# A graph layer's edge loop: one TensorE signal a step instead of four, and relu(h1) ahead of relu(h2)

## The reference

```python
msg_in = jnp.concatenate([node_features[row], node_features[col]], axis=-1)
h = jax.nn.relu(msg_in @ Wm1 + bm1)          # h1, 256 wide
h = jax.nn.relu(h @ Wm2 + bm2)               # h2, 256 wide
messages = h @ Wm3 + bm3
agg = jax.ops.segment_sum(messages, col, num_segments=num_nodes)
...
agg = agg / jnp.clip(count, 1.0)[:, None]
upd = jax.nn.relu(jnp.concatenate([node_features, agg], axis=-1) @ Wn1 + bn1) @ Wn2 + bn2
x = _layernorm(x + (node_features + upd), axis=-1)
```

## Time and profile before

| what | value |
|---|---|
| time, median of 3 runs | 1221.72 us |
| span of the profiled execution | 1422.7 us |
| stage 1, up to the first transpose of the loop | 89 us |
| edge loop in the profiled execution | 1236 us, 391 steps |
| stage 3 in the profiled execution | 97.7 us |
| mean granted TensorE clock | 0.991 |

### The profile page before, as it was taken

One profiled execution on the slowest core, in us unless ns is written; L12 is line 12 of the kernel. 1 busy time (PEld: TensorE's weight loads), 2 busy tenths in 40 slices (PEclk: granted clock), 3 DMA queues, 4 the chain that ended last, 5 costly groups with the idle time before them and its releaser, 6 DMA issues.

```text
span 1422.7 us, 34295 instructions
## 1 busy us (share of the span) xinstructions
PE 1256.0 (88%) x9586; PEld 1169.5 (82%) x9587; DVE 969.2 (68%) x2072; ACT 728.3 (51%) x1392; POOL 772.3 (54%) x814
## 2 busy tenths in 40 slices
PE   6978988888889988998889888999888988899897
PEld 5868888888888888888888888888888888888786
DVE  6856666666666666666666766767676776777676
ACT  3544554554554554554555454545545445455585
POOL 2166666666666665666666656666656666664000
PEclk9999999999999999999999999999999999999999
DMA  9765555455444545555445545454554445555012
GB/s 303 284 222 153 144 146 147 146 146 148 144 147 143 149 147 146 145 145 147 147 144 146 149 144 146 143 150 142 145 147 144 144 144 147 147 143 151 15 65 87
DMA packets 135603, 211.39 MB, mean 149 GB/s; under 512 B 24247, under 2 KB 102669, under 8 KB 134030
## 3 DMA queue, kind: packets, MB, share of 16 engines
q1 hardware_dynamic: 98030, 108.43, 25.5%
q0 software_dynamic: 37536, 102.55, 24.7%
HBM read 188.09 MB, written 22.80 MB: 148 GB/s over the span
## 4 chain that ended last, share of the span: by engine, by line
PE 58%; issue 16%; DVE 6%; another core or an unknown queue 6%; ACT 5%; DVEq 4%; DMA 2%; POOL 1%; SPq 1%; ACTq 0%
PE bank L1407 27%; PE bank L1365 9%; PE bank L1311 5%; PE sums L1328 4%; ACT bank L728 2%; PE sums L1332 2%; PE bank L1438 2%; PE sums L1336 2%; PE sums L1334 2%; ACT h L731 2%; PE sums L1451 1%; DVE h_lo L1098 1%; DVE onehot_t L1013 1%; DVE h L1104 1%
## 5 line engine op out<-in xcount | busy, mean ns | idle before, releaser
L624 POOL DMA_INDIRECT a_edge<-a_table,src_idx x782 | 752.9, 963 | 479.8 <-remote 280.5
L1407 PE MATMUL bank<-w,h 128*128 128x256 f32 x4692 | 655.4, 283 | 93.7 <-issue 92.6
L1407 PEld LDWEIGHTS bank<-w,h 128*128 128x128 f32 x4692 | 595.6, 189 | 116.7 <-issue 116.2
L721 ACT ACTIVATE h_hi<-bank 128x512 fp32r<-128x512 f32 x391 | 234.6, 600 | 453.3 <-remote 360.6
L1098 DVE SCALAR_TENSOR_TENSOR h_lo<-bank,h_hi 128x512 fp32r<-128x512 f32 x391 | 267.6, 685 | 137.5 <-issue 132.5
L1104 DVE SCALAR_TENSOR_TENSOR h<-bank,h 128x512 fp32r<-128x512 f32 x391 | 268.3, 686 | 105.9 <-ACT h L731 53.5
L731 ACT ACTIVATE h<-bank 128x512 fp32r<-128x512 f32 x391 | 234.1, 599 | 135.5 <-remote 62.2
L1365 PE MATMUL bank<-ident,a_edge 128*128 128x128 f32 x1564 | 241.8, 277 | 35.7 <-DVE onehot_t L1013 18.8
L1028 DVE SCALAR_TENSOR_TENSOR onehot<-iota,first_node,dst_col 128x256 fp32r<-128x256 int16 x391 | 187.4, 479 | 88.0 <-issue 86.5
L728 ACT COPY bank<-b_bc 128x512 f32<-128x512 f32 x391 | 234.8, 600 | 23.5 <-DVE h_lo L1098 17.4
L1365 PEld LDWEIGHTS bank<-ident,a_edge 128*128 128x128 f32 x1564 | 177.8, 141 | 54.2 <-DVE onehot_t L1013 30.7
(11 more groups left out here) (186 smaller groups left out, 668.5 us busy)
## 6 DMA issues: line engine op xcount, KB each, us to landing
b_win<-b_table SPq DMA_DIRECT2D x391, 128.0 KB
rel<-rel_dram SPq DMA_DIRECT2D x196, 128.0 KB
a_edge<-a_table,src_idx POOLq DMA_INDIRECT x782
a_table<-work SPq DMA_DIRECT2D x12, 512.0 KB, 4.8
b_table<-work SPq DMA_DIRECT2D x5, 1024.0 KB
b_table<-h SPq DMA_DIRECT2D x4, 1024.0 KB
f_x<-in_x SPq DMA_DIRECT2D x12, 256.0 KB, 6.0
b_table<-a_edge SPq DMA_DIRECT2D x3, 1024.0 KB, 6.1
```

Of the source, the lines that this page charges most:

```text
L624: pool.indirect_dma_start(a_edge[:, b % R * TB + t, :], None, a_table, bass.IndirectOffsetOnAxis(ap=src_idx[:, b * TB + t:b * TB + t + 1], ...
L721: act.activation(h2_hi[:, (k - AHEAD - 1) % U, :, 0:H], bank[H2[(k - AHEAD - 1) % U]][:, :].rearrange("p (t h) -> p t h", t=TB), ACT.Relu) ...
L1407: ins = pe.matmul(to, h1[:, j, a, h * EB + t * P:h * EB + (t + 1) * P], w2[:, b, h, :], start=False, stop=(a == 1 and h == KH - 1), skip_g ...
```

## The change

It does four things. (1) TensorE no longer raises `s_ta`, `s_sg` and `s_w2` in each step; `s_ex`, behind the expansion, is the one signal of a step, and the order of TensorE's queue makes it stand for the transposes of the same step and for the sums and the W2 products of the step before. In the last steps, where no expansion follows, `s_w2` (the last 3) and `s_sg` (the last 6) are still raised. GpSimd now waits for `s_ex`. (2) ScalarE computes relu(h1) of step k first, then puts b2, then computes relu(h2) of step k - 3 (LAG = 3) without a wait of its own. VectorE follows the same order: low part of h1, one-hot for step k + 2, then the one-hot and the low part of h2 of step k - 3. (3) VectorE adds a finished range one step later. (4) On TensorE the branch for further ranges moves from ahead of the expansion to ahead of `begin_range`.

```diff
-                    pool.wait_ge(s_ta, b - R + 1)
+                    pool.wait_ge(s_ex, b - R + 1)
...
 # ScalarE
                 for k in steps(i):
-                    if there(i, k - AHEAD - 1):
-                        act.wait_ge(s_w2, i * U + (k - AHEAD))
-                        act.activation(h2_hi[...], bank[H2[(k - AHEAD - 1) % U]], ACT.Relu).then_inc(s_h2h, 1)
                     if there(i, k):
+                        if isinstance(i, int) and U * i + k < LAG:
+                            put_b2(k)
+                        act.wait_ge(s_ex, i * U + (k + 1))
+                        act.activation(h1[:, k % U, 0, :], bank[k % 2][:, :], ACT.Relu).then_inc(s_h1h, 1)
                         if there(i, k - U):
                             act.wait_ge(s_h2l[k % U], nth(i, k - U))
-                        act.copy(bank[H2[k % U]][:, :], b2_bc)
-                        act.wait_ge(s_ex, i * U + (k + 1))
-                        act.activation(h1[:, k % U, 0, :], bank[k % 2][:, :], ACT.Relu).then_inc(s_h1h, 1)
+                        if not isinstance(i, int) or U * i + k >= LAG:
+                            put_b2(k)
+                    if there(i, k - LAG):
+                        if among_last(i, k - LAG, LAG):
+                            act.wait_ge(s_w2, nth_last(i, k - LAG, LAG))
+                        act.activation(h2_hi[...], bank[H2[(k - LAG) % U]], ACT.Relu).then_inc(s_h2h, 1)
...
 # VectorE, end_range
-                dve.wait_ge(s_sg, i * U + (k + 1))
+                if among_last(i, k, BACK + 1):
+                    dve.wait_ge(s_sg, nth_last(i, k, BACK + 1))
...
 # VectorE: the pair of step k - 3 (make_onehot, h2_lo) moves behind h1_lo(k) and make_onehot_t(k + 2);
-                            with dve.If((word & 2**8) > 0):
-                                end_range(i, k - BACK, word)
+                            with dve.If((word & 2**8) > 0):
+                                end_range(i, k - BACK - 1, word)
...
 # TensorE
-                        ins.then_inc(s_ta, 1)
-                    with pe.If((word & (2**13 - 1)) > 0):
-                        (further ranges of k - BACK - 1; far spans of k)
+                        spans = word & 127
+                        with pe.If(spans > 0):
+                            with pe.Fori(1, within(spans, 1, NFE) + 1):
+                                expand_far(k)
                         expand(b_win[:, k % RB, :], onehot_t[:, k % 2, :], k).then_inc(s_ex, 1)
...
                             with pe.If(word > 2**13 - 1):
+                                sum_all_further(k - BACK - 1, word)
                                 begin_range(k - BACK)
...
-                        other_sums(bank_at(own), (k - BACK) % U, k - BACK).then_inc(s_sg, 1)
+                        ins = other_sums(bank_at(own), (k - BACK) % U, k - BACK)
+                        if among_last(i, k - BACK, BACK + 1):
+                            ins.then_inc(s_sg, 1)
...
-                        ins.then_inc(s_w2, 1)
+                        if among_last(i, k - AHEAD, LAG):
+                            ins.then_inc(s_w2, 1)
```

More of the change, by code:

```diff
@@ L24 @@
 BACK = 5
+LAG = AHEAD + 1
 XB = 7
@@ L269, in gnn_layer @@
         s_h1l = [sem(f"s_h1_lo{k}") for k in range(U)]
-        s_w2 = sem("s_h2_product")
+        s_w2 = sem("s_last_h2_product")
         s_bits = sem("s_banks_written")
@@ L277, in gnn_layer @@
         s_wrap = sem("s_edges_wrapped")
-        s_sg = sem("s_segments_summed")
+        s_sg = sem("s_last_segments_summed")
         s_sgm = sem("s_further_segments_summed")
@@ L398, in there, with among_last, nth_last @@
             return not isinstance(i, int) or 0 <= U * i + k < NBE
+        def among_last(i, k, n):
+            return isinstance(i, int) and U * i + k >= NBE - n
+        def nth_last(i, k, n):
+            return U * i + k - (NBE - n) + 1
         def steps(i, back=BACK):
@@ L627, in _ @@
                                             ).then_inc(s_g[b % R], 16)
-            pool.wait_ge(s_w2, NBE)
+            pool.wait_ge(s_w2, LAG)
             for k in range(2):
@@ L712, in load_far, with put_b2 @@
                                       ).then_inc(s_bf, 16)
+            def put_b2(k):
+                act.copy(bank[H2[k % U]][:, :], b2_bc[:, :, :].rearrange("p t h -> p (t h)"))
             def body(i):
@@ L1091, in body @@
                             make_far_onehot_t(0, j)
-                for k in steps(i, BACK + 1):
+                for k in steps(i, BACK + 2):
                     word = words[k]
[L1094 to L1098, removed]
-                                                 bank[H2[j]][:, :].rearrange("p (t h) -> p t h", t=TB),
-                                                 0.0, h2_hi[:, j, :, 0:H].bitcast(F32),
-                                                 ALU.max, ALU.subtract).then_inc(s_h2l[j], 1)
                     if there(i, k):
@@ L1346, in sum_further, with sum_all_further @@
                 other_sums(bank_at(other), FURTHER, k).then_inc(s_sgm, 1)
+            def sum_all_further(k, word):
+                further = (word >> 7) & 63
+                with pe.If(further > 0):
+                    with pe.Fori(1, within(further, 1, NW - 1) + 1):
+                        sum_further(k)
+                    pe.reg_add(settled, ended, 1)
+                    pe.wait_ge(s_add, settled)
             def begin_range(k):
@@ L1397, in body @@
                             first_sum(bank_at(own), (k - BACK) % U, k - BACK, False)
-                        other_sums(bank_at(own), (k - BACK) % U, k - BACK).then_inc(s_sg, 1)
+                        ins = other_sums(bank_at(own), (k - BACK) % U, k - BACK)
+                        if among_last(i, k - BACK, BACK + 1):
+                            ins.then_inc(s_sg, 1)
+                    elif there(i, k - BACK - 1):
+                        sum_all_further(k - BACK - 1, word)
                     if there(i, k - AHEAD):
```

40 lines of the change are left out of this document (16 added, 24 removed).

## The result

The changed kernel takes **1238.14 us** (1237.69 to 1241.09, four runs), the kernel before beside it 1221.74 (1220.55 to 1224.82). The ratio is 1.0131, with an interval of 1.0113 to 1.0149: slower by 16 us, where 1220 was forecast and 1232 was the upper end.

A forecast was written before the change was run, and what follows sets the result against it. The prediction took TensorE to bound the loop, 2.57 us a step and 1005 us for 391 steps. Its terms summed as 1221.7 - 0 - 0 + 0 - 1 = about 1220 us, with a range of 1198 to 1232.

The forecast's parts named there:

- An addition delays the next step by 0.4 and is made up in it. Cost 0: VectorE adding a finished range one step later: its step needs 1.9 us of 2.57, so the delay costs 0.
- I take 0 and keep 23 for the range: GpSimd's gathers wait for `s_ex`, 0.24 us later: 0 in the running loop, at most 23 us if cold-start latencies hold.
- the last range is added behind TensorE's last sums as before: End of the loop: no cost for the last range; filling and draining the loop saves perhaps 1 us.
- Rival C: Gathers bind at L624, one wait later: 0.06 us a step, 23 us, 1245 us; part, 10 us, likelier, 1232. Chance 0.15.
- a closed ring: Gather slots reused after four steps, 10.28 us: gathers, landing, window load and one-hot take 7.0 us running, 10.2 at start.
- a wait at the transposes: Sign of late gathers in the profile after: TensorE waits at its transposes for one-hot L1013, and that for `b_win`.
- The recording: Inference from two totals: most late TensorE signals come with recording the profile, span 1423 us against 1221.7 timed.
- the prediction's own sign: Profile after: if late signals are the recording's, the profiled span stays near 1423 us, since TensorE records as many instructions.
- its 30 us: Waits in the timed loop: timed median 1221.7 against 1192 us without waits, about 30 us left to give.
- A smooth step: A loop step in which nothing waits, TensorE's work only: 2.57 us, expected to keep the same pieces after the change.
- a gain of 31 us: Estimate for 1173 fewer TensorE signals at the skill page's 26.3 ns, giving 1191 us; the prediction took 0.
- relu(h1) first and relu(h2) later: ScalarE's and VectorE's new orders: one-hot lead 2.4 to 2.7 us, low h2 lead 4.4 to 2.4; gain 0, cost 0.

The follow-up runs named there:

- the second profile of the kernel before: Kernel before, unchanged, profiled again on another visit: span 1422.2 us, with 1424.55 us for the kernel before run beside it.
- the last experiment: Kernel before, with SyncE loading b's window without waiting for the gather and VectorE waiting for it instead: 1203.26 us beside 1224.17, ratio 0.9826.

## Why the prediction was wrong

*The steps that failed.* "An addition delays the next step by 0.4 and is made up in it. Cost 0" is the first. The two additions delay VectorE by 1.1 us and not 0.8, and above all they are not made up: in most steps VectorE waits for its window of b, at the stall above in both that follow. The term was 0; the part, with its test at a range's start, measures 11 us. The second is the gathers: "I take 0 and keep 23 for the range". It measures 6 to 8 us. A small third is "the last range is added behind TensorE's last sums as before": it is added later, and the third stage's first products wait 4.5 us instead of 3.1. Rival C named the gathers, and its 10 us were near, but not its mechanism: TensorE doesn't wait in a closed ring at every step. 0.2 us of later window make VectorE's lateness after a range a bit longer, and it is steps near a range's start that show on TensorE. The forecast that C would appear as a wait at the transposes was wrong for the changed kernel (9.1 us in 6 waits): with the low part of h2 last in VectorE's queue, it appears ahead of the sums.

*Why it could not be seen in the rows.* In the profile before, a step takes 3.16 us and VectorE has 1.2 us to spare in each. At 2.57 it has 0.7, and a gather and a window that land 3.8 us after the gather's issue ends are just too late. The prediction carried VectorE's operation times to the shorter step but not its waits for transfers. It did note that the transfers come closer together, and gave the whole of C 0.15.

*The recording.* Most of the 201 us between profile and timed runs was put down to the recording. That was wrong in its cause, as the run beside the second profile of the kernel before shows, and the prediction's own sign said so first: the profiled span was to stay near 1423 us and is 1236. It was right in its use: the traces of the fast visits have no late signals, the loop of the kernel before with the new orders is 1037 us where the prediction left 1035, and 21 of its 30 us could be had by the last experiment.

*What was right.* A smooth step is still 2.57 us with the same pieces. The signals cost nothing that shows: the parts, orders 0.1%, gathers 0.5 to 0.6%, range 0.9%, add up to 1.5 or 1.6% where the whole is 1.3 to 1.5%, each known to 0.2 or 0.3%, so nothing that can be told is left for them; the signals were not run by themselves. The 26.3 ns an increment of the Trainium skill's page "TensorE: Matmul & The Clock Gate", section "The cost: per-tile semaphore tail", would by the prediction's estimate have been a gain of 31 us, and no run here shows it. relu(h1) first and relu(h2) later cost 0, as worked out, to within 0.3%, even though the lead of 2.4 us is used up wherever VectorE is late.

*Where the later addition hurts.* In the kernel before the two additions fall into the steps before and at a range's start, in the changed one into that step and the next. The excess moves along: in the kernel before with the new orders 11.3 us of it lie in the second step after a range's start, in the changed kernel 9.0 us in the third, and 14.0 in the steps that start a range themselves, instead of 1.9. Where the excess has moved to, the next range often begins: 31 of the 59 starts counted come three or four steps after the last one. These 31 have 0.6 us of excess in the kernel before with the new orders, 9.3 with the range a step later alone, 10.8 of the 14.0 us in the changed kernel (10.9 of 18.5 when it was run again), and 5.9 without the test. So the lateness now falls where TensorE has a new range to begin and a test to make.

*What stays open.* How the 11 us divide between the test, the later step and the end of the loop, since medians and single traces differ, and whether early windows take the loss from the changed kernel as they do from the kernel before.

## What to carry to other kernels

An engine with time to spare on average absorbs a burst only if nothing else makes it wait in between: for each "made up in the next step", list what that engine waits for in that step, and at the shortest step the kernel can reach. If two parts of a change each cost something and both meet the same late engine, look at that engine's wait before you look at the change: here three lines on SyncE and VectorE were worth 21 us in the kernel before, more than the whole change lost. And before reading waits from a profile, hold its own time against the timed runs; when they differ by 16%, its waits are those of another regime.

## What the runs showed of the hardware

**Two speeds of TensorE's instructions.** On the visits over 1400 us TensorE's records (products, weight loads, branches, register operations) come at 16.4 to 16.9 in a microsecond from 300 to 1000 us, 59 to 61 ns each, in all twelve traces, whatever the kernel; in the changed kernel's trace at 1236.2 us it is 19.6, and 20.0 in the 1202.3 us one. The granted clock is 0.99 on both kinds of visit. In the two profiles of the kernel before there, waits for something "remote" are up to 3.8 us long, where the traces of the faster visits have none, and no variant differs from the kernel before by more than 0.3%. What puts a visit into one kind or the other no run here shows. The Trainium skill, "TensorE: Matmul & The Clock Gate", section "Wait — 56ns, not 53.3ns?", gives about 62 ns for each product when hardware decoding is off and the sequencer's software handles it. The figure is near, but it is for products alone, and no run here shows which way the instructions were decoded.

**A wait that ends in time can still cost.** TensorE's branches run ahead of its products: in the changed kernel the branch ahead of the sums (L1402) starts 1.07 us before the first sum in the median step. Where a wait has just let go, such instructions come in the open: 0.08 us for that branch at the stall above, 0.46 for the test at a range's start (746.90 to 747.36) and 0.16 for the register operations behind it.
